# Tokenizer's second synthesis level as TensorE products with gate diagonals, and the quads of tiles 1 and 2 placed around image 0's projections

## What is computed

```python
for _ in range(3):                                   # analysis, three Haar levels
    cur, h, v, d = _dwt2(cur)
    details.append((h, v, d))
rec = cur * sigmoid(cur.reshape(B, -1) @ Wa + ba)    # one gate per image
for (h, v, d), (Wd, bd) in zip(reversed(details), det_params):
    w = softmax(stack([h, v, d]).reshape(B, -1) @ Wd + bd)     # three gates per level and image
    rec = _idwt2(rec, h * w[:, 0], v * w[:, 1], d * w[:, 2])   # synthesis of one level
h = rec
h = h + attention(layernorm(h))
h = h + experts(layernorm(h))
```

## Time and profile before

| | us |
|---|---|
| median of three runs | 1122.88 |
| lowest and highest | 1122.46, 1124.04 |
| the profiled execution | 1127.43 |
| its span | 1125.6 |
| PE, DVE, ACT, POOL busy | 987.4, 681.8, 590.8, 733.0 |
| mean granted clock of PE, as a share | 0.961 |

### The profile page before, as it was taken

One profiled execution on the slowest core, in us unless ns is written; L12 is line 12 of the kernel. 1 busy time (PEld: TensorE's weight loads), 2 busy tenths in 40 slices (PEclk: granted clock), 3 DMA queues, 4 the chain that ended last, 5 costly groups with the idle time before them and its releaser, 6 DMA issues.

```text
span 1125.6 us, 19279 instructions
## 1 busy us (share of the span) xinstructions
PE 987.4 (88%) x7000; PEld 821.7 (73%) x7000; DVE 681.8 (61%) x1505; ACT 590.8 (52%) x1108; POOL 733.0 (65%) x667
## 2 busy tenths in 40 slices
PE   0536986999999989887799999999999999999996
PEld 0213465778778777664688888888888888888885
DVE  5868655899999877666654453454534445344441
ACT  0112223888888887788354444454444544445442
POOL 4454234898998878798377566575665756657554
PEclk9968898999999999897899999999999999999999
DMA  8223688879979967621344655554455544555333
GB/s 223 75 75 110 134 197 135 131 154 148 156 149 149 147 127 146 93 88 38 104 108 72 146 93 104 117 103 109 90 107 118 102 109 89 109 117 99 75 52 38
DMA packets 105951, 127.62 MB, mean 113 GB/s; under 512 B 12288, under 2 KB 92160, under 8 KB 104832
## 3 DMA queue, kind: packets, MB, share of 16 engines
q1 hardware_dynamic: 81280, 92.81, 38.3%
q0 software_dynamic: 24576, 33.57, 18.3%
HBM read 79.67 MB, written 46.14 MB: 112 GB/s over the span
## 4 chain that ended last, share of the span: by engine, by line
PE 47%; POOL 1%; DVE 1%; issue 1%; ACT 0%; DMA 0%; POOLq 0%; DVEq 0%; ACTq 0%
PE y_ps L1378 15%; PE gate_ps L1356 15%; PE value_ps L1356 15%; PE xT_ps L1339 2%; POOL out L1311 1%; POOL x_rows L1301 0%; DVE hidden_lo L1460 0%; DMA x_rows<-normed_scratch,slot_row 0%; DVE xg_lo L1456 0%; DVE top_index L129 0%; DVE top_index_f L1491 0%; DVE hidden L1470 0%; ACT L1421 0%; DVE top L125 0%; DVE work L131 0%
## 5 line engine op out<-in xcount | busy, mean ns | idle before, releaser
L1311 POOL DMA_INDIRECT out<-y_rows,slot_row x128 | 204.9, 1601 | 175.4 <-ACT y_rows L1414 145.0
L1470 DVE TENSOR_TENSOR hidden<-silu_g,value_ps 128x512 f32<-128x512 f32 x128 | 88.0, 688 | 296.2 <-PE value_ps L1356 162.8
L344 POOL TENSOR_TENSOR probs_k<-probs_full,probs_k 128x512 f16<-128x512 f32 x192 | 222.1, 1166 | 51.5 <-ACT probs_k L806 49.2
L1421 ACT ACTIVATE silu_g<-gate_ps 128x512 f32<-128x512 f32 x128 | 76.5, 598 | 273.6 <-PE gate_ps L1356 273.6
L799 ACT ACTIVATE probs_full<-scoresT_ps,log 128x512 f32<-128x512 f32 x192 | 131.0, 683 | 70.7 <-PE scoresT_ps L603 45.5
L1301 POOL DMA_INDIRECT x_rows<-normed_scratch,slot_row x124 | 136.8, 1103 | 42.4 <-issue 37.2
L1378 PE MATMUL y_ps<-w_hi,hidden_hi 128*128 128x256 f32 x512 | 144.9, 283 | 1.2 <-DVE hidden_lo L1460 1.1
L1378 PE MATMUL y_ps<-w_hi,hidden_lo 128*128 128x256 f32 x512 | 144.6, 282 | 0.0
L1378 PE MATMUL y_ps<-w_lo,hidden_hi 128*128 128x256 f32 x512 | 144.5, 282 | 0.0
L806 ACT ACTIVATE probs_k<-probs_full 128x512 f16<-128x512 f32 x192 | 119.5, 623 | 0.0
L1356 PE MATMUL gate_ps<-xg_hi,w_hi 128*128 128x512 f32 x256 | 103.7, 405 | 1.2 <-DVE xg_lo L1456 1.2
(11 more groups left out here) (232 smaller groups left out, 2373.3 us busy)
## 6 DMA issues: line engine op xcount, KB each, us to landing
w_raw<-in_L_ffn_w SPq DMA_DIRECT2D x48, 512.0 KB, 4.1
q_stack<-q_scratch SPq DMA_DIRECT2D x96, 128.0 KB, 4.9
k_stack<-k_scratch SPq DMA_DIRECT2D x96, 128.0 KB, 7.9
x_tile<-in_x SPq DMA_DIRECT2D x4, 1024.0 KB, 5.1
h_scratch<-rec_tile SPq DMA_DIRECT2D x4, 1024.0 KB, 3.9
hacc<-h_scratch SPq DMA_DIRECT2D x4, 1024.0 KB, 5.5
q_scratch<-q_hi SPq DMA_DIRECT2D x16, 256.0 KB, 2.2
q_scratch<-q_lo SPq DMA_DIRECT2D x16, 256.0 KB, 2.5
```

Source lines behind the costliest of these rows:

```text
L344: G.tensor_tensor(probs(b, 1, n), pf[N % 3][:].rearrange("p (a q) -> p a q", a=4 if n % 3 == 2 else 2), probs(b, 0, n), ALU.subtract).then ...
L1311: G.indirect_dma_start(out=rows, out_offset=bass.IndirectOffsetOnAxis(ap=sel.idx[:, c, j, e:e + 1], axis=0), in_=ys[U % 2][:, j, :], in_of ...
L1421: A.activation(sg[ft % 2][:], GP[ft % 2][:], ACT.Silu).then_inc(silu_done, 1)
L1470: V.tensor_tensor(hf[ft % 2][:], sg[ft % 2][:], VP[ft % 2][:], ALU.mult).then_inc(hf_done, 1)
```

## The change

The synthesis level l = 1 leaves DVE for every tile. ACT makes six further diagonals `diag1` (with the gates of level 1) ahead of the old six. PE's new `level(t)` multiplies them with the bands of 128 columns: four groups of four products, which land interleaved in one PSUM bank (`LB`, in `scores_ps1`). ACT's new `level_left(t)` evicts the bank to `low` of 512 columns, and only then is `low_done` counted. DVE's second and last level now counts `low1_done`. The quads and the gate matmuls get another order on PE and ACT: two quads of tile 1 before image 0's transposes and two after them, Q and K of image 0, then tile 2's gates, its level and two quads, then V of image 0 and the transposes of image 1, and then one quad, tile 3's gates, one quad and tile 3's level. Tile 3's quads keep their ticks. The core of the diff:

```diff
-    CUT = (-18, -6)
+    CUT, MID = (-18, -6), -13
+            diag1 = tb("gate_diag1", [P, 6, P])
+        LB = SR[1][:].rearrange("p (r i c j) -> p i j r c", r=2, i=2, c=D // 4)
...
+            def level(t):
+                pe.wait_ge(low1_done, t + 1)
+                pe.wait_ge(diag1_done, 6 * (t + 1))
+                if t == 0:
+                    pe.wait_ge(wt_lo, 2)
+                for i in range(2):
+                    for j in range(2):
+                        terms = ((ident[:], low[t % 2][1][:]), (diag1[:, 3 * i], band[t % 2][1][:, 0]), (diag1[:, 1 + 3 * j], band[t % 2][1][:, 1]),
+                                 (diag1[:, 2 + 3 * ((i + j) % 2)], band[t % 2][1][:, 2]))
+                        for m, (lhsT, src) in enumerate(terms):
+                            ins = pe.matmul(LB[:, i, j], lhsT, src, start=(i + j + m == 0), stop=(i + j == 2 and m == 3), skip_group_check=True)
+                ins.then_inc(lev_ps, 1)
...
             tile(0)
-            synths(0)
+            level(0)
+            for k in range(3):
+                synth(0, k)
+            tile(1)
+            synth(0, 3)
             pe.wait_ge(wt_lo, 3)
+            level(1)
+            synth(1, 0)
+            synth(1, 1)
             ticks(FIRST, CUT[0])
-            synths(1)
-            ticks(CUT[0], CUT[1])
-            synths(2)
+            synth(1, 2)
+            synth(1, 3)
+            ticks(CUT[0], MID)
+            tile(2)
+            level(2)
+            synth(2, 0)
+            synth(2, 1)
+            ticks(MID, CUT[1])
+            synth(2, 2)
+            tile(3)
+            synth(2, 3)
+            level(3)
             pe.wait_ge(rw1_in, 16)
             ticks(CUT[1], LAST + 1)
...
             def diagonals(t):
                 act.wait_ge(gate_done, t + 1)
                 for k in range(6):
+                    A.activation(diag1[:, k], ident[:], ACT.Copy, scale=(gate, ngate)[k // 3][:, 4 + k % 3:5 + k % 3]).then_inc(diag1_done, 1)
+                for k in range(6):
                     A.activation(diag[:, k], ident[:], ACT.Copy, scale=(gate, ngate)[k // 3][:, 7 + k % 3:8 + k % 3]).then_inc(diag_done, 1)
+
+            def level_left(t):
+                act.wait_ge(lev_ps, t + 1)
+                A.activation(low[t % 2][0][:].rearrange("p r c -> p (r c)"), SR[1][:], ACT.Copy).then_inc(low_done, 1)
...
-                for l in (2, 1):
+                for l in (2,):
...
-                    v.wait_ge(low_done, t)
+                    v.wait_ge(low1_done, t)
```

More of the change, by code:

```diff
@@ L265, in front @@
         zsum = OP
+        low1_done, lev_ps, diag1_done = sem("low1_done"), sem("lev_ps"), sem("diag1_done")
+        LB = SR[1][:].rearrange("p (r i c j) -> p i j r c", r=2, i=2, c=D // 4)
         wps = [SR[0][:].rearrange("p (k d) -> p k d", k=2), SR[1][:].rearrange("p (k d) -> p k d", k=2), MA[:]]
@@ L768, in _ @@
                 ins.then_inc(wt_ps, 1)
[L769 to L773, removed]
-            tile(0)
-            synths(0)
+            tile(0)
+            level(0)
[3 more added lines that the diff above has]
+            synth(0, 3)
             pe.wait_ge(wt_lo, 3)
+            level(1)
+            synth(1, 0)
+            synth(1, 1)
             ticks(FIRST, CUT[0])
-            synths(1)
-            ticks(CUT[0], CUT[1])
-            synths(2)
+            synth(1, 2)
[10 more added lines that the diff above has]
+            level(3)
             pe.wait_ge(rw1_in, 16)
@@ L909, in _ @@
                 A.activation(WT[m][0][:], wps[i], ACT.Copy).then_inc(wt_hi, 1)
[L910 to L915, removed]
             gates(0)
             diagonals(0)
-            synths_left(0)
+            level_left(0)
+            for k in range(3):
+                synth_left(0, k)
+            gates(1)
+            synth_left(0, 3)
+            diagonals(1)
+            level_left(1)
+            synth_left(1, 0)
+            synth_left(1, 1)
             act.wait_ge(c_in, 16 * 3)
@@ L922, in _ @@
             ticks(FIRST, CUT[0])
-            synths_left(1)
-            ticks(CUT[0], CUT[1])
-            synths_left(2)
+            synth_left(1, 2)
+            synth_left(1, 3)
+            ticks(CUT[0], MID)
+            gates(2)
+            diagonals(2)
+            level_left(2)
+            synth_left(2, 0)
+            synth_left(2, 1)
+            ticks(MID, CUT[1])
+            synth_left(2, 2)
+            gates(3)
+            synth_left(2, 3)
+            diagonals(3)
+            level_left(3)
             ticks(CUT[1], LAST + 1)
@@ L1086, in tile @@
                     c.step(V.tensor_tensor(dst[:, :, :, 0], a_, b_, ALU.add))
[L1087 to L1091, removed]
+                    c.wait()
+                    V.tensor_tensor(dst[:, :, :, 1], a_, b_, ALU.subtract).then_inc(low1_done, 1)
             def ticks(t0, t1):
```

## The result

The changed kernel takes 1134.15 us (median of 4 runs, 1133.64 to 1136.11), beside 1122.67 (1121.60 to 1124.04) for the kernel before on the same chip. The ratio is 1.0091, 95% interval 1.0072 to 1.0110. It is slower, and the forecast of 1135.6 was 1.45 us off. Its profiled execution took 1134.59 us, with a span of 1132.8, where the prediction had about 1138; that of the kernel before had 1125.6.

A forecast was written before the change was run, and what follows sets the result against it. TensorE bounds the kernel from about 200 us; before that it waits in a start-up chain, the only part touched. Terms 8.5 - 1.9 + 6.1 gave +12.7 us on the median 1122.88: 1135.6 us, range 1126 to 1143.

The forecast's parts named there:

- (a): Prices: a level's products take 3.5 us on TensorE warm, 7.0 at half clock, then 1.0 to the next quad.
- (b): Tile 0: level starts cold at 41, quads run from 48.0 to 61.9, +1.7 us.
- (c): Tile 1: level and two quads hide in TensorE's idle 19 us; transposes at 80.95, GpSimd's tile 3 split at 90.4.
- (d): Tile 2's gates beside GpSimd's split, then level and two quads ahead of image 0's V projection: V 8.5 us later.
- (e): From image 0's V projection to tile 3's gates: TensorE now warm, 1.9 us shorter, gates at 132.9.
- (f): Tile 3's gates to tick 0 (image 0's first scores): quad, eviction, diagonals and level in series, 6.1 us longer.
- Sum: Start of the kernel up to tick 0: 8.5 - 1.9 + 6.1 makes tick 0 12.7 us later.
- Partly absorbed: Rival: TensorE's wait for negmax_lo at 184.50 swallows up to 7.2 us; +5.5, 1128.4 us; chance 0.10.
- Mild: Rival: GpSimd's split and tile 2's gates miss each other, TensorE stays warm in (f); +4.8, 1127.7 us; chance 0.20.
- A shift of tick 0 should reach the end unchanged: After tick 0: waits up to 184.50 answer to things made after tick 0, so the whole 12.7 us carries through.
- signs of being wrong: Level much under 3.5 us, GpSimd's split starting after tile 2's gates, or a shorter stretch after tick 0.
- Faster: Rival: q_lo, ready earlier, sets the V projection; tick 0 up to 6 us earlier, 1117 us; chance 0.06.

The follow-up runs named there:

- e4: Changed kernel, but GpSimd starts tile 3's split only when VectorE has finished tile 2's level l = 2; 1128.75 us, ratio 1.0043.
- x1: Kernel before, level still on VectorE, with image 0's projections and image 1's transposes ahead of tile 2's gates and quads; 1120.23 us, ratio 0.9978.
- x2: x1's order, but with the level as products on TensorE; 1126.55 us, ratio 1.0033 to the kernel before.
- e1: Changed kernel's products kept, but quads and gate matmuls in the order of the kernel before; 1134.56 us, ratio 1.0087.
- e5: e1 with only tile 1's level moved ahead of image 0's transposes; 1129.31 us, ratio 1.0056 to the kernel before.
- e6: e4's held split, plus V of image 0 and image 1's transposes ahead of tile 2's level and quads; 1130.27 us, ratio 1.0045.
- x3: x1 with tile 3's gate matmul moved one quad earlier, behind two quads instead of three; 1120.10 us, ratio 0.9959 to the kernel before.

## Why the prediction was right, step by step

**(a) prices.** Right. A warm level, PE's timeline of the changed kernel at tile 1:

```profile
64.14 0.46 PE L656 MATMUL scores_ps<-low,ident 128*128 128x128 f32 x2 [2.54 <-ACT gate_diag L849]
64.44 0.83 PE L656 MATMUL scores_ps<-band,gate_diag 128*128 128x128 f32 x6
65.11 0.39 PE L656 MATMUL scores_ps<-low,ident 128*128 128x128 f32 x2
```

Groups of eight instructions start 0.89 us apart (65.11, 66.00, 66.90), and the level takes 3.6 (3.5 predicted). Tile 2's first groups stand 1.87 and 1.70 apart (granted clock 0.50 in 105 to 109), and its level took 6.2, the value that I had taken between the bounds. From the start of tile 1's level to its first quad took 4.50 us (64.14 to 68.64), as the sum had it (3.5 and 1.0); of the 1.0, no row gave the drain of 0.3 and the wake-up of 0.1 by themselves. The estimate from the Trainium skill's TensorE: Matmul & The Clock Gate, "Back-to-back issue gap" (81 ns, 2.6 us a level) is not what these rows show: 0.11 us an instruction at a granted clock of 1.00.

**(b), (c) tiles 0 and 1.** Right: quads of tile 0 from 47.39 (48.0), POOL's split of tile 2 at 62.40 (62.8 by the sum), transposes at 80.15 (80.95). These levels do hide in PE's idle time: 4.38 us of it were left ahead of the transposes. Tile 3's split began at 91.48 and 88.51 in the two profiles (90.4).

**(d) tile 2's gates to V, +8.5.** It measured +9.7 (118.55) and +9.3. The step under-priced the collision: level(2) was to start at 103.2 and started at 105.04 and 105.18. I had carried tile 0's 8.7 us over, but POOL was there in smaller operations; here it is in its largest, of 1024 columns, and DVE's sums ahead of the gates can be hit as well, which I left out. By the rule of the Trainium skill, SBUF — State Buffer, "SBUF: two separate sides", whichever instruction starts first holds the shared pair and the other blocks fully; the traces agree in both directions (1.68 for nine columns on DVE, 3.49 for POOL's 1.89). e4 shows the size: 6.6 us, where the prediction had 4.4.

**(e) V to the gates of tile 3, -1.9.** It measured -1.7 (118.55 to 134.22). PE idled 8.11 us ahead of the gate matmul, 8 predicted.

**(f) gates of tile 3 to tick 0, +6.1.** It measured +4.1 against the first profile of before and +5.8 against the second, of which a stretch ran warm that was cold in the first. The quad was 5.4 (5.9), the level, which I had put at 4.5, was warm at 3.6, and from `synth(3,0)` to tick 0 it took 8.7 (9.2). Two windows of the changed kernel tell why, the fields as in the earlier trace rows:

```profile
134.00:136.00 2.00, 2.00 (x4) 0.97 (x5) 1.26 (x10) 0.21 (x1) 0.00 (x0) 0.50 0.00 0
...
142.00:144.00 2.00, 2.00 (x18) 2.00 (x19) 0.00 (x0) 1.54 (x6) 0.00 (x0) 1.00 0.66 266
```

After 8 us of idling the quad begins at a granted clock of 0.50, and the level behind it runs at 1.00.

**Sum.** +12.7 predicted, +12.04 and +13.2 measured at tick 0. The two errors, 1 us too little in (d) and up to 2 too much in (f), partly cancel. **Partly absorbed** was the rival that came in by a part. The wait for `negmax_lo` shrank from 7.23 and 6.48 to 5.20 and 5.45, which takes 1 to 2 us. Of **Mild**, a small part: the split and the gates met in both profiles, but in (f) the level was warm (3.6) behind a cold quad (5.4).

**Behind tick 0.** "A shift of tick 0 should reach the end unchanged" did not hold in the profiles, and one of the prediction's own signs of being wrong came in. From tick 0 to the end of the span the kernel before takes 982.5 and 981.1 us, the changed kernel 977.7 and 977.5. So 3.6 to 5 us of the shift are gone at the end, 1 to 2 of them at `negmax_lo`; where the others go was not followed. Over all thirteen profiles this stretch takes 977 to 982.5 us, and x1 and x2, 5.0 us apart at tick 0, end 0.9 apart in their profiled executions, though 6.3 in their medians. The spans of the two kernels differ by 7.2 and 9.6 us, less than the 12.7 forecast. That the forecast of the time, made on the median, came out within 1.45 us is thus in part luck: the mechanism ahead of tick 0 is shown row by row, its size at the end only by the medians and the ratio. **Faster** fell with the order and the collision: q_lo was ready at 107.3, only 1.6 us earlier than the 108.87 at which V took it before, and V stood behind two quads by then.

The experiments also correct the picture behind the sum. The prediction adds terms along one spine. There is a second one, tile 1's last quad, POOL's split of tile 3, the power, tile 3's products, which e1, e5 and e6 ran into. It was hidden in the changed kernel, and this is why repairs of 8.2 and 6.6 us together give 7.1. Why x1's V, 9.4 us earlier, brings 2.6 us at most at tick 0 is shown only in part: x3 shows that the gate matmul by itself gives nothing, because the diagonals behind the last quad's eviction are over no sooner. What the next bound behind these would be was not tried. Nor was a version of the changed kernel with tile 3's diagonals ahead of the last quad's eviction (139.44), though DVE's `ngate` was ready 3 us before it.

## What to carry to other kernels

In a ramp that is a chain through several engines, moving work off an engine gains only if that engine's next product was waited for. Count what the move puts in series (here diagonals, products, an eviction), and what it puts ahead of an operation that was ready. Check each repair for the chain next below: here two repairs of one ramp did not add. A shift in an engine's start also moves what it collides with, so an estimate for contention should say which operations meet, not only how many.

## What the runs showed of the hardware that was not expected

The end of a collision of DVE and POOL can be the same while its parts are not: in two executions of one program DVE's gates took 11.3 and 8.1 us, its last sums 2.2 and 3.79 us each, and the level behind them began at 105.04 and 105.18. Two executions do not show that this is a rule. The collision also hits `hn`, a tensor-scalar operation with one tensor input: two of 256 columns took 3.71 us in e1, e4, e5 and e6 beside the split, and 0.73 in the changed kernel at 79.36, where POOL was between two splits.
